# Second cross attention of a perceiver block: order of the queries, the first scores and the state space kernel's products

## The reference

```python
Q = (x_text @ Wq).reshape(Bb, Tt, H, DH)                  # H = 4 heads of DH = 32
K = (x_vision @ Wk).reshape(Bb, Gg, H, DH)                # 4096 keys in each of 2 batches
scores = jnp.einsum('bthd,bghd->bhtg', Q, K) / np.sqrt(DH)
topv, topi = jax.lax.top_k(scores, K_TOP)                 # the 32 largest of 4096
probs = jax.nn.softmax(topv, axis=-1)
attn_mean = zeros.at[..., topi].set(probs).mean(axis=1)   # mean over the heads
c_t = attn_mean @ (x_vision @ Wv)
...                                                       # s4d: a state space layer whose kernel
K = 2.0 * jnp.einsum('dn,dnl->dl', dC, powers).real       # (256 channels, 256 steps) needs no x
```

## Time and profile before

| | |
|---|---|
| three runs | 1115.05 us median, 1112.32 to 1117.0 |
| profiled execution, its own time | 1113.37 us |
| its span (first to last instruction) | 1112.1 us, granted TensorE clock 0.903 |
| busy: PE, DVE, ACT, POOL | 945.5, 825.8, 652.7, 300.2 us |
| second cross attention's start | about 668.2 us from the span's start |
| its exact path | VectorE, 704.3 to 735.9 us |

### The profile page before, as it was taken

One profiled execution on the slowest core, in us unless ns is written; L12 is line 12 of the kernel. 1 busy time (PEld: TensorE's weight loads), 2 busy tenths in 40 slices (PEclk: granted clock), 3 DMA queues, 4 the chain that ended last, 5 costly groups with the idle time before them and its releaser, 6 DMA issues. The chain is left out here.

```text
span 1112.1 us, 20953 instructions
## 1 busy us (share of the span) xinstructions
PE 945.5 (85%) x7732; PEld 588.5 (53%) x7732; DVE 825.8 (74%) x1713; ACT 652.7 (59%) x1044; POOL 300.2 (27%) x332
## 2 busy tenths in 40 slices
PE   5996949999999999998698998538788888899697
PEld 5975814444444444444466885324455556735455
DVE  4776778999999999980446987888877776278347
ACT  3432405878887887877245435149999999401212
POOL 1000078889800000000120532004555553000001
PEclk9999957999999999999789997557688999898989
DMA  5868651222222322210402307202165225780000
GB/s 181 297 239 289 247 145 46 80 76 79 77 82 74 82 76 82 75 31 1 117 1 86 100 16 204 85 1 62 30 172 144 59 61 161 232 198 12 1 0 20
DMA packets 99321, 111.83 MB, mean 101 GB/s; under 512 B 26658, under 2 KB 75731, under 8 KB 99219
## 3 DMA queue, kind: packets, MB, share of 16 engines
q1 hardware_dynamic: 96802, 109.50, 32.9%
q10 hardware_dynamic: 2416, 0.99, 0.4%
HBM read 80.95 MB, written 29.43 MB: 99 GB/s over the span
## 5 line engine op out<-in xcount | busy, mean ns | idle before, releaser
L835 ACT ACTIVATE pT<-bank 128x512 f32<-128x512 f32 x512 | 278.4, 597 | 95.1 <-PE bank L752 74.1
L857 DVE TENSOR_REDUCE rmax<-bank 128x2 f32<-128x1024 f32 x256 | 307.3, 1223 | 28.1 <-PE bank L720 27.2
L764 PE MATMUL bank<-pT,V 128*17 128x256 f32 x2048 | 161.8, 388 | 4.7 <-ACT oT L841 4.5
L1736 PE MATMUL bank<-K1s,qs 97*128 97x512 f32 x256 | 119.7, 570 | 50.7 <-ACT below L1845 30.9
L752 PEld LDWEIGHTS bank<-qs,ks 49*128 49x128 f32 x1024 | 78.1, 187 | 113.1 <-ACT pT L835 99.6
L752 PE MATMUL bank<-qs,ks 49*128 49x256 f32 x1024 | 130.5, 333 | 2.3 <-ACT pT L835 0.5
L720 PE MATMUL bank<-ks,qs 49*128 49x512 f32 x512 | 111.0, 429 | 16.3 <-DMA ks<-k_parts_d 9.1
L2008 POOL TENSOR_TENSOR total<-total,work 128x1024 f32<-128x1024 f32 x40 | 94.9, 2380 | 34.6 <-ACT work L1854 33.7
L1736 PEld LDWEIGHTS bank<-K1s,qs 97*128 97x128 f32 x256 | 55.6, 229 | 66.8 <-ACT below L1845 32.0
L1906 DVE MAX8 cand<-work 128x8 f32<-128x128 f32 x384 | 76.6, 283 | 0.0
L764 PEld LDWEIGHTS bank<-pT,V 128*17 128x17 f32 x2048 | 34.5, 95 | 63.5 <-ACT pT L835 42.7
(11 more groups left out here) (468 smaller groups left out, 1804.3 us busy)
## 6 DMA issues: line engine op xcount, KB each, us to landing
k_parts_d<-kparts SPq DMA_DIRECT2D x48, 512.0 KB
ks<-k_parts_d SPq DMA_DIRECT2D x381, 64.0 KB, 2.2
K1s<-k_parts_d SPq DMA_DIRECT2D x96, 128.0 KB
cn<-in_ctx SPq DMA_DIRECT2D x32, 384.0 KB, 3.5
cx<-in_ctx SPq DMA_DIRECT2D x16, 384.0 KB, 5.3
w<-in_L_ffn_w SPq DMA_DIRECT2D x32, 128.0 KB, 2.3
w2e<-in_L_ffn_w SPq DMA_DIRECT2D x16, 128.0 KB, 2.5
W<-in_L_xattn_W SPq DMA_DIRECT2D x2, 1024.0 KB, 7.8
```

The source lines that it names most:

```text
L764: t = pe.matmul(bank[32 * c:32 * c + VW, 7, a * S:(a + 1) * S], V[:, b * NCH + 4 * g + c, h, :], pT[:, (at + 2 * (c // 2) + a) % 8, c % 2 ...
L835: p_made.up(act.activation(pT[:, at % 8, :], bank[:, 4 + at % 3, :], ACT.Exp))
L857: max_read.up(dve.tensor_reduce(rmax[p % 2][:, :, qt, c], bank[:, b0:b0 + 2, :], AX.X, ALU.max))
L1736: m = pe.matmul(bank[:, b0 + c, :], qs1[0:NROW1, b * H1 + h, q], K1s[h][0:NROW1, keys], start=True, stop=(what == "new"))
```

## The change

1. TensorE no longer makes sixteenths 0 to 3 ahead of the turned tokens. All sixteen stand behind the count of tile 0 (`g == K_TURN`, 5), in one bank (7), with a wait for ScalarE's copy after each four.
2. TensorE makes the query products of heads 0 and 1, then two pieces of tile 0, head 2's product, two more pieces, head 3's product. Each head's first new piece waits for that head's `q1_low` alone; piece (0,2), which uses banks 4 and 5, waits for heads 0 and 1.
3. ScalarE's `query_high` and VectorE's `query_low` move in the same way between the copies and the candidates of tile 0.
4. ScalarE makes `minus`, just ahead of the four kernel copies, which stand ahead of `mark_below` of tile 0.

The diff:

```diff
--- before.py
+++ after.py
@@ -1543,38 +1543,38 @@
         xh_made1.up(pool.tensor_tensor(xh_[:, :, :], xh_[:, :, :], norm_in[:, 1:2, :].to_broadcast([P, NT, D]), ALU.add))
 
     def prep_tensor():
-        pe.wait_ge(*powers_made.at(1))
-        for at in range(4):
-            kernel_sixteenth(at, 2)
         pe.wait_ge(*ln_made.at(4 * 4))
         turn_tensor(tokens_of(xt_))
         pe.wait_ge(*wq3_made.at(1))
         pe.wait_ge(*xT_made.at(10))
-        for h in range(H1):
-            for kt in range(2):
-                t = pe.matmul(bank[0:MASK_ROW, 4 + h, :], wq3[:, kt * H1 + h, :, :].rearrange("p a d -> p (a d)"), xT[:, kt, :],
-                              start=(kt == 0), stop=(kt == 1))
-            q1_made.up(t)
+
+
+    def query_product(h):
+        for kt in range(2):
+            t = pe.matmul(bank[0:MASK_ROW, 4 + h, :], wq3[:, kt * H1 + h, :, :].rearrange("p a d -> p (a d)"), xT[:, kt, :],
+                          start=(kt == 0), stop=(kt == 1))
+        q1_made.up(t)
+
+    def query_high(h):
+        act.wait_ge(*q1_made.at(h + 1))
+        q1_high.up(act.activation(qs1[0:MASK_ROW, h:NB * H1:H1, :], bank[0:MASK_ROW, 4 + h, :].rearrange("p (b s) -> p b s", b=NB),
+                                  ACT.Identity, scale=1.0 / math.sqrt(D1)))
+
+    def query_low(h):
+        low = slice(2 * D1, MASK_ROW)
+        dve.wait_ge(*q1_high.at(h + 1))
+        q1_low.up(dve.scalar_tensor_tensor(qs1[low, h:NB * H1:H1, :], bank[low, 4 + h, :].rearrange("p (b s) -> p b s", b=NB),
+                                           1.0 / math.sqrt(D1), qs1[low, h:NB * H1:H1, :], ALU.mult, ALU.subtract))
 
     def prep_scalar():
         norm_scalar(3)
         turn_scalar(4)
-        copy_kernel(0, 2)
         norm_scalar(4)
-        for h in range(H1):
-            act.wait_ge(*q1_made.at(h + 1))
-            q1_high.up(act.activation(qs1[0:MASK_ROW, h:NB * H1:H1, :], bank[0:MASK_ROW, 4 + h, :].rearrange("p (b s) -> p b s", b=NB),
-                                      ACT.Identity, scale=1.0 / math.sqrt(D1)))
 
     def prep_vector():
         norm_vector(xt_, x)
         vec.wait()
         norm_vector(xh_, xt_)
-        low = slice(2 * D1, MASK_ROW)
-        for h in range(H1):
-            dve.wait_ge(*q1_high.at(h + 1))
-            q1_low.up(dve.scalar_tensor_tensor(qs1[low, h:NB * H1:H1, :], bank[low, 4 + h, :].rearrange("p (b s) -> p b s", b=NB),
-                                               1.0 / math.sqrt(D1), qs1[low, h:NB * H1:H1, :], ALU.mult, ALU.subtract))
 
     run(prep_sync, prep_pool, prep_vector, prep_scalar, prep_tensor)
 
@@ -1657,7 +1657,7 @@
             quads[4 * s + k] = (grp, n)
 
 
-    K_FROM, K_BANK = 4, 7
+    K_BANK, K_TURN = 7, 5
 
     def best_sync():
         tm_in.up(sp.dma_start(tm8[:, :], ins["mask_BxS_bf1"].rearrange("b (t p) -> p (b t)", p=P)), 16)
@@ -1725,6 +1725,8 @@
             at = nth[what, t, k]
             q = slice(qt * P, (qt + 1) * P)
             b0 = 2 * (at % 3)
+            if what == "new" and t < H1 and k == 0:
+                pe.wait_ge(*q1_low.at(t + 1))
             if what == "new":
                 pe.wait_ge(*k1_in[h][k].at(64 * (b + 1)))
             else:
@@ -1772,24 +1774,30 @@
             c0_made.up(m)
 
         pe.wait_ge(*qone_made.at(1))
-        pe.wait_ge(*q1_low.at(1))
-        for k in range(4):
-            if k == 1:
-                pe.wait_ge(*K_copied.at(1))
-            if k == 2:
-                pe.wait_ge(*q1_low.at(H1))
-            piece("new", 0, k)
-        pe.wait_ge(*minus_made.at(1))
+        query_product(0)
+        query_product(1)
+        piece("new", 0, 0)
+        piece("new", 0, 1)
+        query_product(2)
+        pe.wait_ge(*q1_low.at(2))
+        piece("new", 0, 2)
+        piece("new", 0, 3)
+        query_product(3)
+        pe.wait_ge(*powers_made.at(1))
         for g in range(4 * (NTL + 1)):
             s, k = g // 4, g % 4
             for what in pieces_of(s, k):
                 piece(*what)
             if s and k == (s < NTL):
+                if s == 1:
+                    pe.wait_ge(*q1_low.at(H1))
                 sum_over(s - 1)
-            if g < 12:
-                if g % 4 == 0:
-                    pe.wait_ge(*K_copied.at(g // 4 + 1))
-                kernel_sixteenth(K_FROM + g, K_BANK)
+            if g == K_TURN:
+                for n in range(16):
+                    if n and n % 4 == 0:
+                        pe.wait_ge(*K_copied.at(n // 4))
+                    kernel_sixteenth(n, K_BANK)
+                pe.wait_ge(*minus_made.at(1))
             if g - 1 in quads:
                 weigh_quad(*quads[g - 1])
             if g in quads and g - 1 in quads:
@@ -1864,8 +1872,14 @@
             aT_made.up(act.copy(xT[:, at % 2, :], bank[:, 6, :]))
 
         act.preload_act_table_set("natural_log_exp_and_others")
-        for k in range(4):
-            copy_scores(0, k)
+        query_high(0)
+        query_high(1)
+        copy_scores(0, 0)
+        copy_scores(0, 1)
+        query_high(2)
+        copy_scores(0, 2)
+        copy_scores(0, 3)
+        query_high(3)
         for s in range(NTL + 1):
             for k in range(4):
                 for what, t, piece in pieces_of(s, k):
@@ -1873,6 +1887,10 @@
                         copy_scores(t, piece)
                     else:
                         exps(t, piece)
+                if 4 * s + k == K_TURN:
+                    minus_made.up(act.activation(minus[:, :], identb[:, :], ACT.Identity, scale=-1.0))
+                    for quarter in range(4):
+                        copy_kernel(quarter, K_BANK)
                 if 1 <= s < NTL:
                     if k % 2:
                         mark_below(s - 1, k - 1, 2)
@@ -1888,8 +1906,6 @@
                         sum_best(s - 1)
                         log_sum(s - 1)
                         exp_bias(s - 1)
-                if s < 3 and k == 3:
-                    copy_kernel(s + 1, K_BANK)
                 if 4 * s + k in quads:
                     copy_quad(*quads[4 * s + k])
         exps(LAST, 3)
@@ -1968,11 +1984,14 @@
             c0_copied.up(dve.tensor_scalar(c0[:, grp, :], bank[:, 7, grp % 2 * 256:grp % 2 * 256 + DC], tmask[:, grp:grp + 1],
                                            None, ALU.mult))
 
-        minus_made.up(dve.tensor_scalar(minus[:, :], identb[:, :], -1.0, None, ALU.mult))
+        query_low(0)
+        query_low(1)
         for s in range(NTL + 1):
             for k in range(4):
                 if s < NTL:
                     candidates(s, k)
+                if s == 0 and k % 2:
+                    query_low(2 + k // 2)
                 if k == (s < NTL) and 1 <= s <= NTL:
                     over_to_sbuf(s - 1)
                     settle(s - 1)
```

## The result

| | before | changed |
|---|---|---|
| runs | 1114.92 us median of 4 (1112.32 to 1117.0) | 1100.45 us median of 4 (1098.97 to 1105.35) |
| ratio to before | | 0.9879, 95% interval 0.9842 to 0.9916 |
| span of the profiled execution, granted clock | 1112.1 us, 0.903 | 1099.5 us, 0.916 |

Later comparisons, run beside the experiments, make the gain smaller than this first one: the changed kernel, run again, had 1102.01 us beside 1109.73 for 25 runs of before, ratio 0.9933 (0.9909 to 0.9957). All 84 runs of the kernel before that I have lie between 1102.1 and 1118.1, median 1111.4; the ten runs of the changed kernel have a median of 1102.0.

A forecast was written before the change was run, and what follows sets the result against it. VectorE was taken to set the time in 704 to 736 us, ScalarE from 800 on. Gains of 4.8 up to the cast and 3.3 after the exact path summed to 8.1 us: forecast 1106.2 us, range 1102.3 to 1112.

The forecast's parts named there:

- the prediction's own upper end of 10.8: Whole kernel: the largest summed gain, 10.8 us, giving 1102.6 us.
- Step 1: Start of the second cross attention: turn at 672.75 taking 1.97 us at low clock, first query product 1.0 us earlier.
- Step 2: Two query products, then scores: VectorE's first maxima at 682.8 instead of 687.13, 4.3 us earlier.
- the central case: First scores: product 0 at the low clock, what follows at the high; first maxima at 682.8.
- Step 3: Cast of tile 0's count: VectorE's 1.90 us wait vanishes, keys come in time; gain up to the cast 4.8 us.
- Step 4: Sixteen sixteenths beside the exact path: last copy at 725, exact path until 731.3, 6 us of cover left.
- Step 5: After the exact path: waits and kernel copies vanish, gain 3.3 us, between 0 and 4.3.
- my upper end of 4.3: After the exact path: 4.3 us gained if all waits and copies come back.
- Rival A: After the exact path: waits stay, owed to a low clock; gain 4.8 us alone, 1108.6 to 1110.3; chance 0.11.
- rival B: Start of the stage: clock stays low throughout; gain 3.0 us, 1110.4 to 1112.1; chance 0.11.
- Rival C: Exact path: sixteenths outlast it and delay TensorE's first cut piece; 10 us slower, 1123 to 1125; chance 0.05.

The follow-up runs named there:

- before_again: The kernel before without an edit, for a second profile; 1112.14 us, ratio 1.0023.
- minus_dve: The changed kernel with the negated identity made by VectorE again, between the query lows of heads 0 and 1 and its first maxima; 1103.91 us.
- keep_four: The changed kernel with sixteenths 0 to 3 again ahead of the turned tokens, the other twelve beside the exact path; 1102.91 us.
- warm: The changed kernel with three products of constants, whose result nothing reads, ahead of the turned tokens while VectorE normalizes; 1099.13 us.
- again: The changed kernel without an edit; 1102.01 us, ratio to before 0.9933.
- noexact_after: The changed kernel with tile 0's count set to its usual value, so no tile takes the exact path; 1095.48 us.
- start_only: The changed kernel with the sixteenths back in their old places, early first scores and ScalarE's identity kept; 1112.4 us, ratio to before 1.0040.
- kernel_only: The kernel before with all sixteenths beside the exact path, old query order and VectorE's negated identity kept; 1105.07 us, ratio to before 0.9956.
- last_four: The changed kernel with sixteenths 12 to 15 and their copy back behind the exact path, one after each of steps 8 to 11; 1103.09 us.
- noexact_before: The kernel before with the count set to its usual value, so no tile takes the exact path; 1079.15 us, ratio to before 0.9716.

## Why the prediction missed

**The base.** The sum was made from a profiled execution of 1113.37 us and a median of 1115.05 from three runs. The median of 84 runs is 1111.4. In the first profile the stretch behind mark 2 is 3.5 us longer than in before_again, the same program. The end of the program shows such a difference most plainly. The 16.2 us behind the last mark, in the profiles of before and of minus_dve, which has 159.15 us there where before has 162.12 with the same instructions:

```profile
949.98:958.08 8.10, 5.53 (x23) 4.74 (x24) 4.89 (x5) 3.40 (x5) 0.00 (x0) 0.70 0.62 226
...
958.08:966.18 8.10, 8.10 (x51) 8.02 (x50) 0.00 (x0) 2.34 (x4) 0.00 (x0) 0.87 0.58 156
```

```profile
940.15:948.25 8.10, 5.52 (x27) 4.81 (x28) 4.90 (x5) 3.58 (x6) 0.00 (x0) 0.79 0.72 256
...
948.25:956.35 8.10, 8.10 (x57) 7.99 (x56) 0.00 (x0) 2.75 (x5) 0.00 (x0) 1.00 0.76 210
```

The clock is 0.70 and 0.87 in the one, 0.79 and 1.00 in the other, and 3 us of difference remain to the end. My range allowed for unknown costs of the steps and took the base as known to 1.7 us; with a kernel whose runs lie 16 us apart, this was a failing choice. 1111.4 less the sum of 8.1 would have been 1103.3.

Of the 5.75 us between the forecast and 1100.45, 2.9 are the base (1106.2 + 8.1 = 1114.3 against 1111.4), 1.9 are the sum (8.1 against 10.0), and 0.95 are left. Some of it is luck: with 1111.4 as the base, the prediction's own upper end of 10.8 gives 1100.6, which still misses the first four runs by 0.15 us and holds the 1102.0 of all ten.

**The sum: 8.1 against 10.0 in the profiles.** By steps:

- Step 1, right: turn at the low clock, 1.97 us, 2.15 us earlier counted from the stage's start (1.87 forecast). That removing the four gains nothing by itself (keep_four), and that the warm clock is worth 2.4 us to the first maxima (warm against again), are the two ends of the step. The reason that I gave, that the sixteenths kept TensorE at work and the clock up, is only half of what the trace of before shows: the clock fell to 0.50 while TensorE made them without a break, and was back when the turn came.

```profile
670.00:672.00 2.00, 2.00 (x97) 2.00 (x89) 1.66 (x7) 0.20 (x1) 0.96 (x2) 0.50 0.83 244
...
672.00:674.00 2.00, 1.99 (x90) 1.77 (x83) 1.97 (x7) 0.00 (x0) 0.00 (x0) 0.65 0.53 160
```

- Step 2, the central case, its size off by 0.9: first maxima 13.66 after the start against 14.54. The turn came 0.28 us sooner than forecast (VectorE's last normalization took 1.65 instead of 1.88), the first product was seen after 3.46 instead of 3.7, since the clock came back within it, and from the second product to the first maxima it took 1.53 instead of 2.0. Part of this is chance: noexact_after, with the same instructions, has 14.69. That the negation held the first maxima before was misread, as shown above.
- Step 3, right: 15.24 from maxima to cast against 15.4, no wait for the count. That the keys would be there in time was wrong (waits up to 1.26 us) and cost nothing. start_only shows that the start can be lost at this place, though about half of its wait has another reason.
- Step 4, right in kind: the chain from count to last copy took 725.54 - 693.67 = 31.9 us instead of 30.4, mostly the gap of 1.84 at 699.76, and the cover left was 4.7 instead of 6. noexact_after shows that it is this cover. Rival C is refuted for this data (its end of the sixteenths, 749.3, comes to 749.1 when added up again, which changes nothing).
- Step 5 is the term of the sum that failed by most: 4.5 against 3.3, above my upper end of 4.3. Up to tile 1's mark 1.9 came against 1.7; from there to tile 2's mark 2.6 against 1.65. The rows of before that I left out:

```profile
753.99 0.47 ACT L1832 ACTIVATE lsum<-ssum 128x1 f32<-128x1 f32 x1
...
762.71 0.15 DVE L1934 CAST over_i<-bank 1x1 int32<-1x1 f32 x1 [2.38 <-PE bank L1747]
...
764.58 2.09 ACT L1845 ACTIVATE below<-work,steep_thr,steep 128x2048 bf16<-128x2048 f32 x1 [0.18 <-issue]
```

The stall before 755.32 is bracketed with 0.85, but from the start of the small operation ahead of it (753.99) to 755.32 it is 1.33 us, where the changed kernel has 0.11 (745.96 to 746.07), so the stall costs 1.2. The second copy's 0.8 (759.40 to 760.21) came as forecast. And VectorE's wait of 2.38 at 762.71 for the next count also ended on ScalarE's path: mark 2 came 1.48 after the copy at 763.10, 0.93 after its like in the changed kernel. I had counted the wait at 748.38 and not its successor. The last 0.55 lie between the cast and the mark, where VectorE has 1.29 us of `issue` before and 0.67 in the changed kernel (1.24 and 0.67 in their second profiles); why this gap is longer stays open.

Rival A (only the start gains) and rival B (low clock throughout) did not come; kernel_only and last_four speak against A, the clock of 1.00 in 678 to 680 against B. Against A there is also the clock itself from mark 0 to mark 2, which was no higher in the changed kernel, 0.64 against 0.68. Before and changed:

```profile
736.18:764.58 28.40, 22.10 (x301) 13.44 (x302) 21.65 (x100) 25.50 (x29) 3.12 (x4) 0.68 0.05 10
```

```profile
730.20:754.12 23.92, 17.16 (x43) 8.20 (x43) 21.18 (x100) 22.73 (x26) 2.84 (x4) 0.64 0.17 53
```

## What to carry to other kernels

Two changes in front of one wait are not worth the sum of their single gains: in one comparison, by its ratios, the moved filler alone gained 4.9 us, both together 7.4, and the early start alone lost 4.4. Before a part is called worthless from such a run, look at what the cut-down version waits for: the early start alone met an occupied bank (3.71 us) that neither the kernel before nor the changed one meets. Work put beside a long operation is free for just as long as that operation really runs, so ask which input decides that. Before summing a few microseconds, learn how far the runs of the same program lie apart, from more than one profile, and put that into the range.

## What the runs showed of the hardware that I had not expected

- Two profiles of programs that are identical over a stretch of 162 us differ there by 3 us, most of it behind 16 us in which the granted clock was 0.70 and 0.87 in one, 0.79 and 1.00 in the other; over a stretch of 185 us, by up to 4.
- A bf16 negation of 128 x 128 on VectorE took 2.27, 1.65 and 1.21 us (before, minus_dve, before_again), each time until the running tensor add of GpSimd had ended, and 0.20 us in noexact_before, where it fell between two adds (the first ended at 685.18, the second began at 685.26); on ScalarE it took 0.31.
- Three products of constants during a gap of TensorE brought the following turn from 1.97 to 1.09 us in both profiles in which they stood, but the products after it to 3.65 us in one and 5.34 in the other.
- While TensorE made sixteenths without a break (2.00 us busy of 2.00 in 670 to 672 of before), the granted clock was 0.50.
